# Cross-attention in a decoder layer: value products directly behind the next scores, clamps in the step of their exponential

## The reference

```python
x = x + attn(_layernorm(x), gamma, Wq, Wkv, Wo)             # 16 heads of 128, one shared key/value head, causal
x = x + xattn(_layernorm(x), ctx_2048, mask, Wq, Wk, ...)   # 16 heads of 16 over 1500 context rows
x = x + ffn(_layernorm(x), gate_w, val_w, out_w, ...)       # silu gate, width 1024, inputs quantised per row
```

```python
q, k, v = proj(hs, Wq, bq), proj(at, Wk, bk), proj(at, Wv, bv)
scores = clip(einsum('bhsd,bhtd->bhst', q, k) / 4, -50, 50)
scores = clip(where(attend, scores, -10000.), -50, 50)
probs = softmax(scores)
ctx = einsum('bhst,bhtd->bhsd', probs, v)
delta = rs * (ctx @ Wo.T + bo);  delta = layernorm(delta) * ln_gamma + ln_beta
```

## Time and profile before

| | |
|---|---|
| median of 3 runs | 1415.37 us (1415.36 to 1417.24) |
| profiled execution | 1415.76 us, its span 1414.0 us |
| busy | TensorE matmul 98%, VectorE 69%, ScalarE 51%, GpSimd 32% |
| granted TensorE clock | mean 0.996 |

### The profile page before, as it was taken

How to read it: one execution, slowest core, us unless ns; L and a number is a source line. 1 busy time by engine, 2 the same in 40 slices (tenths; PEclk the granted TensorE clock), 3 DMA queues, 4 the chain that set the end, 5 groups by cost and what they waited for, 6 DMA issues and landing times.

```text
span 1414.0 us, 55254 instructions
## 1 busy us (share of the span) xinstructions
PE 1387.4 (98%) x25185; PEld 1173.2 (83%) x25195; DVE 969.1 (69%) x1888; ACT 715.5 (51%) x940; POOL 445.9 (32%) x401
## 2 busy tenths in 40 slices
PE   8999999999999999999999999999999999999997
PEld 6787887786788888888888888888888888888874
DVE  5677676665246677677776767677776767677776
ACT  3545445444355555555455555555555555555540
POOL 4333333222323333324324233333333233333310
PEclk9999999999999999999999999999999999999999
DMA  9100001000121121211212121111212122111100
GB/s 263 26 1 31 1 1 31 1 31 1 60 61 46 32 79 50 61 49 46 65 32 65 32 79 51 59 49 46 65 32 68 34 72 64 47 49 46 50 3 7
DMA packets 38923, 66.77 MB, mean 47 GB/s; under 512 B 3718, under 2 KB 36931, under 8 KB 38691
## 3 DMA queue, kind: packets, MB, share of 16 engines
q1 hardware_dynamic: 38690, 63.24, 15.3%
HBM read 61.40 MB, written 1.84 MB: 45 GB/s over the span
## 4 chain that ended last, share of the span: by engine, by line
PE 71%; DVE 2%; issue 0%; POOLq 0%; POOL 0%; DVEq 0%
PE proj_ps L1324 20%; PE proj_ps L1315 19%; PE score_ps L1342 14%; PE sum_ps L1367 12%; PE side_ps L1402 2%; PE side_ps L1416 1%; PE side_ps L1384 1%; PE side_ps L1409 1%; DVE amax L1194 0%; DVE hidden L1226 0%; DVE sig L1236 0%; DVE hidden L1237 0%; PE side_ps L1391 0%; DVE exps L1133 0%; DVE totals L1155 0%
## 5 line engine op out<-in xcount | busy, mean ns | idle before, releaser
L1085 ACT ACTIVATE exps<-score_ps 125x1792 f32<-125x1792 f32 x192 | 320.4, 1669 | 431.2 <-PE score_ps L1342 431.2
L1133 DVE TENSOR_SCALAR exps<-exps,top 125x896 f32<-125x896 f32 x384 | 262.0, 724 | 18.1 <-ACT exps L1085 17.5
L1342 PE MATMUL score_ps<-spread,keys 32*125 32x112 f32 x6144 | 218.9, 279 | 0.0
L1124 DVE COPY vals<-proj_ps 125x512 f32<-125x512 f32 x192 | 129.4, 688 | 110.1 <-PE proj_ps L1324 109.6
L1367 PEld LDWEIGHTS sum_ps<-exps,vals 125*32 125x32 f32 x12288 | 163.1, 110 | 47.1 <-issue 34.1
L1342 PEld LDWEIGHTS score_ps<-spread,keys 32*125 32x125 f32 x6144 | 184.8, 183 | 15.4 <-issue 0.3
L1367 PE MATMUL sum_ps<-exps,vals 125*32 125x56 f32 x12288 | 191.7, 215 | 0.0
L1028 POOL TENSOR_TENSOR low<-raw_early,high 128x500 fp32r<-128x500 f32 x64 | 100.6, 1582 | 216.4 <-PE proj_ps L1315 215.9
L1028 POOL TENSOR_TENSOR low_early<-raw_early,high_early 128x500 fp32r<-128x500 f32 x62 | 104.4, 1702 | 176.3 <-PE proj_ps L1315 176.3
L1077 ACT ACTIVATE keys<-proj_ps,b_k 128x500 f32<-128x500 f32 x192 | 129.9, 676 | 23.6 <-PE proj_ps L1315 21.7
L293 POOL TENSOR_TENSOR swapped<-swapped,sin 128x448 f32<-128x448 f32 (+1 forms) x72 | 88.6, 1232 | 133.2 <-ACT swapped L514 133.2
(11 more groups left out here) (167 smaller groups left out, 2373.1 us busy)
## 6 DMA issues: line engine op xcount, KB each, us to landing
raw_early<-in_ctxT SPq DMA_DIRECT2D x64, 500.0 KB, 4.0
raw<-in_ctxT SPq DMA_DIRECT2D x32, 500.0 KB, 3.6
w_q<-in_attn_Wq SPq DMA_DIRECT2D x4, 512.0 KB, 8.4
w_o<-in_attn_Wo SPq DMA_DIRECT2D x1, 2048.0 KB, 20.7
out<-y_out SPq DMA_DIRECT2D x16, 112.0 KB, 2.3
rows<-in_x SPq DMA_DIRECT2D x1, 1344.0 KB, 16.5
raw_early<-in_ffn_gate_wT SPq DMA_DIRECT2D x1, 1024.0 KB, 10.4
raw_early<-in_ffn_val_wT SPq DMA_DIRECT2D x1, 1024.0 KB, 5.1
```

The source lines that it names most:

```text
L1085: nc.scalar.activation(exps[t % 2][:, :, :, :].rearrange("p h r n -> p r h n"), score_ps[0:TILE, :, 0:2 * QW].rearrange("p r (h n) -> p r ...
L1124: nc.vector.tensor_copy(vals[r][:, 2 * q:2 * q + 2, :, 0:HD], proj_ps[q][0:TILE, :].rearrange("p (k h d) -> p k h d", k=2, d=HD))\
L1133: nc.vector.tensor_scalar(tile, tile, LIMIT_LO, top[:, n, at:at + 1], ALU.max, ALU.min)\
L1342: ins = nc.tensor.matmul(score_ps[0:TILE, r, to:to + HE * S], keys[c % 2][32 * r:32 * r + 32, k, (at + half) * TILE:(at + half + 1) * TILE ...
```

## The change

Two programs of block b get another order. No instruction is added or removed, and no semaphore.

1. TensorE: `add_up` of the step before comes directly behind `scores`, ahead of the side matmuls and the pieces. Before, it was the last thing of the step.
2. VectorE: `limit` of step t is in step t, behind the tail's step (but ahead of it in the steps of `AFTER`) and ahead of the copies of values. Before, it stood at the head of step t + 1. `read_sums` moves with it: of the sequence before to step 0, of the first sequence to step BN, each behind the clamps of that step. The extra clamps behind the loop fall away, since the last step now has its own.

```diff
--- before.py
+++ after.py
@@ -1263,19 +1263,16 @@
                 tail = {} if first else tail_steps(i - 1, False)
                 for t in range(NT):
                     c, half = divmod(t, 2)
-                    for k in range(2):
-                        if t:
-                            limit(i, t - 1, k)
-                        elif not first:
-                            limit(i - 1, NT - 1, k)
-                    if t == 1 and not first:
-                        read_sums(i - 1, 1)
-                    if t == BN + 1:
-                        read_sums(i, 0)
                     if t in tail and t not in AFTER:
                         tail[t]()
                     if last and t == BN + 3:
                         divide(i, 0)
+                    for k in range(2):
+                        limit(i, t, k)
+                    if t == 0 and not first:
+                        read_sums(i - 1, 1)
+                    if t == BN:
+                        read_sums(i, 0)
                     for q in range(2) if half == 1 and not (last and c == PC - 1) else ():
                         if q == 1 and t in tail and t in AFTER:
                             tail[t]()
@@ -1291,8 +1288,6 @@
             for i in range(1, LAST):
                 body(i, False, False)
             body(LAST, False, True)
-            for half in range(2):
-                limit(LAST, NT - 1, half)
             read_sums(LAST, 1)
             for t, step in tail_steps(LAST, False).items():
                 if t:
@@ -1429,6 +1424,10 @@
                 for t in range(NT):
                     c, half = divmod(t, 2)
                     scores(i, t, not first or t >= 1)
+                    if t:
+                        add_up(i, t - 1, not first or t - 1 >= BN)
+                    elif not first:
+                        add_up(i - 1, NT - 1, True)
                     if t in tail and t not in AFTER:
                         tail[t]()
                     if not (last and c == PC - 1):
@@ -1441,10 +1440,6 @@
                         spare(3)
                     if t == NT - 1 and not first:
                         tail[NT]()
-                    if t:
-                        add_up(i, t - 1, not first or t - 1 >= BN)
-                    elif not first:
-                        add_up(i - 1, NT - 1, True)
 
             for p in range(4):
                 piece(0, p, 0, cold=True)
```

## The result

The changed kernel takes **1430.49 us** (median of 4 runs, 1429.12 to 1431.95) against 1415.36 (4 runs, 1414.54 to 1417.24): ratio 1.0105, 95% interval 1.0093 to 1.0118. Slower by 1.05%, as forecast in sign; 7.5 us under the forecast 1438. The profiled execution took 1430.76 us with a span of 1429.0, 15.0 over the span of before.

A forecast was written before the change was run, and what follows sets the result against it. TensorE's own list of work was taken to bound block b. Step 4 (9.2), step 8 (8.3), step 10 (4.2) and the end (1) sum to 22.7 us on the profiled 1415.76, 0.4 over the median: 1438 us, range 1419 to 1445.

The forecast's parts named there:

- Part 1: TensorE's new order: changes of tile shape cost net 0, bounded by 40 us either way over 191 steps.
- The rival of cheaper changes: TensorE, each step: key pieces cheaper to enter from value products than scores, up to 0.21 us, 1398 us; chance 0.09.
- Cover: VectorE's clamps in a plain step finish 1.8 us before their value products come due; tail steps eat into that.
- Step 8: GpSimd's subtraction starts inside the first clamp and holds the second; value products wait 0.59 us, 14 pairs, 8.3 us.
- Step 4: GpSimd's subtraction now falls inside the first clamp and holds the second; value products wait 0.61 us, 15 pairs, 9.2 us.
- Step 10: Clamps come late behind the quantisation, not held by GpSimd; value products wait 0.3 us, 14 pairs, 4.2 us.
- The end: Last pair: the first sequence's division goes ahead of limit(9), delaying value products; net +1 us, between -2 and +3.
- The sum: All waits in block b and the last pair together: 22.7 us added, giving 1438 us.
- one is held: Rival: only one of steps 4 and 8 is held; 1429 us without step 4, 1430 without step 8; chance 0.22.
- my 2.2: VectorE, ahead of step 4's clamps: L1184 follows the projection's read by 2.2 us, between 1.5 and 2.79.

The follow-up runs named there:

- experiment 6: Changed kernel with clamps ahead of silu in steps 8 and 9, inside step 10's quantisation, its subtraction later, last pair's division behind limit(9): 1415.72 us, ratio 1.0000 against before.
- experiment 9: Changed kernel plus one 12-column VectorE instruction directly ahead of the first clamp in steps 4 and 8, kind varied every four pairs: 1438.76 us.
- experiment 10: Changed kernel plus tensor_scalar instructions of varied width and output type directly ahead of the first clamp in steps 4 and 8, varied every three pairs: 1428.12 us.
- experiment 5: Changed kernel with step 10's clamps inside the quantisation, behind its first instruction, and GpSimd's subtraction there behind the quantisation: 1425.89 us, ratio 1.0074 against before.
- experiment 3: Changed kernel with GpSimd's subtraction of step 8 waiting until both clamps of that step are done: 1420.18 us, ratio 1.0030 against the kernel before.
- Experiment 1: Kernel before with VectorE's new order alone, TensorE's order as it was: 1414.45 us, ratio 0.9992 against the kernel before.

## Why the prediction was right and where it was wrong

**Part 1, right.** Changes of shape at 0: chain lengths equal, and experiment 6 within 0.02 us a pair. The rival of cheaper changes falls. The traces also show why the order makes no difference. From the start of the last matmul of one kind to the first of the next it took 0.31 us behind key pieces, 0.21 behind value pieces, 0.20 behind scores and 0.14 behind value products, in both orders (medians between 500 and 1300 us of both traces): the time went by the kind that was left, not by the one that followed.

**Cover, right.** That every plain step keeps 1.8 us and only 4, 8 and 10 are tight: ten of twelve steps kept their length.

**Step 8, right; a size a little off.** Measured against the next scores (865.28), half 0 started 0.24 ahead (worked out: 0.25), the subtraction 0.07 behind (0.07), the second batch of value products 2.10 behind (2.12). The step lost 0.64 instead of 0.59. The prediction priced the later start of the second half alone. Measured are the hole of 0.42 us and the 0.21 by which two batches of 0.60 exceed an unbroken 0.99, together 0.63. 14 x 0.64 = 9.0 against 8.3.

**Step 4: the step that failed.** The prediction said that the subtraction "now lies inside half 0 as in step 8", and so half 1 is held: 0.61 us in 15 pairs, 9.2 us. The times were right: half 0 began 0.36 ahead of the scores (worked out 0.37), the subtraction 0.07 behind (0.09). The inference was wrong. Falling inside half 0 is not enough; it was held 0 times in 15. Step 8 has SCALAR_TENSOR_TENSOR L1237 directly ahead of the clamps, step 4 the tensor_scalar L1202, 256 columns wide. Experiments 9 and 10 turned the outcome around by changing that neighbour; the moment, which shifts with it, did not decide. Had I asked what stands directly ahead of half 0 in the one step where it was held, and in the two where it was not, the difference was there to be seen, though not what it means. In the kernel before it is L1202 in step 10, and in steps 8 and 4:

```profile
857.05 0.69 DVE L1237 SCALAR_TENSOR_TENSOR hidden<-sig,hidden 112x512 f32<-112x512 f32 x1
...
836.99 0.28 DVE L1202 TENSOR_SCALAR xq<-z 112x256 bf16<-112x256 f32 x1
```

**Step 10, right.** 0.31 against 0.29; the step of A(10) carries it, and experiment 5 gives it back. Half 0 began 0.44 us behind the scores (worked out 0.46); the first value products were 0.20 late, not 0.15, since they started 0.15 us behind the end of half 0 and not 0.08.

**The end, right in size** (+0.8 against +1) and by the cause given: the value products of step 9 waited 1.02 us (worked out 1.0), those of step 10 2.13 us. The granted clock fell behind them. Both kernels have in the last pair one stretch of 3.4 us at half (the 1.2 GHz level), here after (start and end, length, busy time of TensorE, its weight loads, VectorE, ScalarE and GpSimd, then the clock, DMA share, GB/s):

```profile
1393.00:1396.40 3.40, 3.40 (x60) 2.39 (x49) 1.48 (x4) 0.00 (x0) 0.00 (x0) 0.50 0.02 5
```

and before:

```profile
1378.60:1382.00 3.40, 3.40 (x72) 2.96 (x72) 1.46 (x4) 0.00 (x0) 0.00 (x0) 0.50 0.02 5
```

So it makes no part of the difference between these two traces.

**The sum.** 9.0 for step 8, 4.4 for step 10, 0 for step 4, 0.8 for the end, 0.3 from the first step of each pair (0.02 each), and 0.5 ahead of pair 1, nearly all of it in block a, whose code is the same: 15.0, the difference of the spans. The forecast had 22.7. That the time still fell inside the range is owed to the range's width, not to step 4. Without the failed 9.2 the forecast would have been 1429, which is the rival "one is held" without step 4; its two variants had 0.22 together. Its own sentence named the doubt ("step 4 rests on my 2.2"), but doubted the wrong thing: the 2.2 was right (measured 2.17).

## What to carry to other kernels

When two engines contend, matching start times do not make two places alike: compare what stands directly ahead of the contended instruction before carrying a hold from one to the other. Work that was held for free in one order must be priced again when its consumer moves nearer, here 1.68 us of half 1 that cost nothing three microseconds ahead of its value products. And on a TensorE that is 98% busy, moving products of one kind past another gained nothing, since the changes of tile shape cost the same in either order; the order that leaves the most cover is the better one.

## What the runs showed of the hardware

**Who gets its turn between two clamps.** The 896-column tensor_scalar on VectorE and the GpSimd subtraction don't run together: whichever waits, its length shows it (half 1 1.68 us instead of 0.68, or the first subtraction 1.96 to 2.77 instead of 1.25). If the subtraction came in half 0, it got its turn between the halves when something small, a wait, or the SCALAR_TENSOR_TENSOR stood directly ahead (L1237: 14 of 14 in step 8 of after; 12 columns: 24 of 24 in step 4 and 8 together in experiment 9, 6 of 6 in 10; with a wait behind 256 columns 3 of 3). It had to wait for both halves when a tensor_scalar of 256 or 2 x 128 columns ran right into half 0 (15 of 15 in step 4 of after, 15 of 15 in experiment 10). That reads as a row of wide tensor_scalars that VectorE runs through without letting go. It is an explanation that fits these counts and was put down before experiment 10; the mechanism in the chip is not shown by it, and two places below do not fit it. The page "SBUF — State Buffer" of the Trainium skill (Who interferes with whom) says that such instructions exclude each other and that the first to issue holds the ports. The trace agrees with the first. The second alone would have let the waiting subtraction in between two instructions in step 4 too, where it stood back 15 times in 15.

**Open.** In step 10 the subtraction comes 0.21 us into L1202, which has the small L1200 directly ahead, and yet VectorE kept its turn through L1202 and both clamps, 14 of 14. By the rule above it should have been let in behind L1202. Step 4 of the kernel before is a second such place: the subtraction came 0.04 us into its L1202 of 256 columns, behind L1200 again, and waited for L1202 and both clamps in 14 of 15 pairs (its first subtraction 2.54 us). So at most the rule holds for a subtraction that comes inside half 0. Where between 12 and 256 columns (or one and two of 128) the change lies was not tried either.

**The end of the kernel at two levels of clock.** The trace of after and that of experiment 10 have the stretch of 3.4 us at the 1.2 GHz level in the last pair, and take 96.4 us from the last pair to the end. Experiments 3 and 9 have the same order there and the upper level, 2.4 GHz, to the end, and take 95.2. Up to the last scores the steps of the last pair agree within 0.04 us in all four; the 1.2 us lie behind them, where the stretch is. So the stretch costs 1.2 us. Experiment 1 has no such stretch either, and its end is 94.0 us against 95.6 of before; what of these 1.6 us is the clock's and what the clamps' new order was not taken apart. Sixteen runs of the kernel before on one chip fall into two groups: ten between 1414.46 and 1415.32 us at a mean granted clock of 0.997 to 0.998, and six between 1416.75 and 1417.06 at 0.994 to 0.995. A difference below 3 us in this kernel should not be read without that number.
